# A graph layer on one core: where x is loaded and the bias added, the closing matmuls, and the order of the first sums and of layer 2's products

## The reference

```python
sums = segment_sum(edge_attr, src, n)
counts = segment_sum(ones, src, n)
agg = sums / maximum(counts, 1)[:, None]
combined = concatenate([x, agg, u[batch]], axis=1)    # 256 + 64 + 128
h = relu(combined @ W1 + b1)                          # 512
y = h @ W2 + b2                                       # 256
out = layernorm(x + y)
```

## Time and profile before

| | |
|---|---|
| median of 3 runs | 831.62 us (831.08 to 832.5) |
| profiled execution | 830.44 us |
| its span | 828.5 us |
| busy: PE, PEld | 763.8, 715.1 us |
| busy: DVE, ACT, POOL | 711.5, 539.7, 402.8 us |
| DMA | 156.37 MB, mean 189 GB/s |

### The profile page before, as it was taken

One profiled execution on the slowest core, in us unless ns is written; L12 is line 12 of the kernel. 1 busy time (PEld: TensorE's weight loads), 2 busy tenths in 40 slices (PEclk: granted clock), 3 DMA queues, 4 the chain that ended last, 5 costly groups with the idle time before them and its releaser, 6 DMA issues. The chain is left out here.

```text
span 828.5 us, 31441 instructions
## 1 busy us (share of the span) xinstructions
PE 763.8 (92%) x11398; PEld 715.1 (86%) x11399; DVE 711.5 (86%) x2317; ACT 539.7 (65%) x1128; POOL 402.8 (49%) x410
## 2 busy tenths in 40 slices
PE   9889999999989989998989978999999998899995
PEld 4689888888879888888888878999999997899995
DVE  8999999899988977987888707999999997799995
ACT  1356655666656646555656557888888885588886
POOL 3066666667666666656666660000000001598994
PEclk9999999999999999999999999999999999899999
DMA  6355555556656555555556448888888889711111
GB/s 206 130 193 195 197 188 195 201 179 203 200 182 202 184 187 184 190 187 185 189 187 181 161 151 278 267 262 260 265 262 258 265 259 242 171 53 61 63 62 63
DMA packets 74034, 156.37 MB, mean 189 GB/s; under 512 B 10851, under 2 KB 51044, under 8 KB 73239
## 3 DMA queue, kind: packets, MB, share of 16 engines
q1 hardware_dynamic: 57096, 102.33, 41.5%
q0 software_dynamic: 16896, 53.54, 17.2%
HBM read 95.47 MB, written 60.37 MB: 188 GB/s over the span
## 5 line engine op out<-in xcount | busy, mean ns | idle before, releaser
L604 POOL DMA_INDIRECT sorted_rows<-payload,idx x264 | 290.5, 1101 | 190.7 <-ACT payload L654 105.5
L867 PE MATMUL ps<-attr_buf,perm 128*128 128x198 bf16 x3168 | 308.8, 253 | 12.6 <-issue 8.4
L867 PEld LDWEIGHTS ps<-attr_buf,perm 128*128 128x128 bf16 x3168 | 287.8, 97 | 25.3 <-issue 18.7
L654 ACT CAST payload<-ps 128x792 bf16<-128x792 f32 x264 | 211.6, 832 | 146.0 <-PE ps L867 101.5
L1164 DVE TENSOR_SCALAR perm<-place_of,pos 128x512 bf16<-128x512 int16 x792 | 242.9, 365 | 23.3 <-PE ps L867 14.0
L1254 DVE TENSOR_SCALAR onehot<-node_of,sup 128x256 bf16<-128x256 int16 x838 | 183.3, 282 | 37.8 <-DMA sup<-sorted_rows 19.3
L949 PE MATMUL ps<-sup,onehot 128*128 128x64 bf16 (+1 forms) x6192 | 199.9, 193 | 5.2 <-issue 2.2
L949 PEld LDWEIGHTS ps<-sup,onehot 128*128 128x128 bf16 x6192 | 195.9, 97 | 9.2 <-issue 7.4
L624 POOL TENSOR_TENSOR xs<-xs,b_all 125x256 f32<-125x256 f32 x50 | 37.9, 782 | 203.8 <-DMA xs<-in_x 203.8
L722 ACT ACTIVATE apart<-node_of,sup 128x256 bf16<-128x256 int16 x194 | 96.6, 498 | 31.2 <-PE ps L949 30.2
L794 PE MATMUL ps<-xt,w1x 128*128 128x125 f32 x800 | 100.2, 279 | 2.9 <-ACT xt L659 2.5
(11 more groups left out here) (150 smaller groups left out, 606.8 us busy)
## 6 DMA issues: line engine op xcount, KB each, us to landing
sup<-sorted_rows SPq DMA_DIRECT2D x129, 396.0 KB, 4.0
attr_buf<-in_edge_attr SPq DMA_DIRECT2D x43, 576.0 KB
xs<-in_x SPq DMA_DIRECT2D x5, 1120.0 KB
out<-weights_z SPq DMA_DIRECT2D x25, 224.0 KB
x_stage<-in_x SPq DMA_DIRECT2D x47, 112.0 KB
sorted_rows<-payload,idx POOLq DMA_INDIRECT x264
pre<-jump_d SPq DMA_DIRECT2D x1, 1560.0 KB
pre<-first_d SPq DMA_DIRECT2D x1, 780.0 KB
```

The source lines that it names most:

```text
L604: pool.indirect_dma_start(out=sorted_rows, out_offset=bass.IndirectOffsetOnAxis(ap=idx[:, n:n + 1], axis=0), in_=payload[s][:, :], in_offs ...
L654: nc.scalar.copy(payload[s][:, :].rearrange("p (r w) -> p r w", w=PART), slots_p[s % PSUM_BUFS]).then_inc(s_pay, 1)
L867: last = nc.tensor.matmul(slot_p[s % PSUM_BUFS][r].rearrange("p (h f) -> p h f", f=PLANE), places, parts(a, t * CB + s), start=(t == 0 and ...
```

## The change

x goes into `xs` in twelve pieces of four columns and one of two. Each is loaded behind the super loads of one of SP's turns 3 to 15, whose loop is written out for it. POOL adds b2 to a piece as soon as it has landed, all 50 columns ahead of its first low part. The eight closing matmuls have one column each. PE runs 17 matmuls with zeros over 252 columns of bank 7 that hold no table, once two means are taken. Hidden sum 0 stands ahead of the means of banks 4 and 5, and the second split behind those of 2 and 3. Layer 2 computes the high products of both columns first and the low ones last, with one start and one stop for the bank.

```diff
--- before.py
+++ after.py
@@ -94,6 +94,8 @@
 PAIR_BUFS = 8
 HOT_BUFS = 4
 BODY = 2 * PAIR_BUFS
+UNUSED = 512 - (BUCKETS - (PAIR_BANKS - 1) * BANK_COLS) * ROW
+FILLERS = 17
 SUP_TURNS = SUPER_PAIRS // PAIR_BUFS
 PLACES_AT_ONCE = 4
 assert 2 * SUPER_PAIRS - SUP_TURNS * BODY <= PLACES_AT_ONCE
@@ -116,12 +118,12 @@
 LOOKS = -(-(BATCHES - SOON) // LOOK)
 assert LOOKS + 3 <= CHUNKS
 
-X_COLS = 10
+X_TURN = 3
+X_COLS = 4
 X_PIECES = COLS // X_COLS
 X_PIECE = X_COLS * DIM
-B2_AHEAD = 3
 Z_BUFS = 3
-assert X_PIECES * X_COLS == COLS and X_COLS % 2 == 0 and X_COLS // 2 >= B2_AHEAD
+assert X_TURN + X_PIECES + 1 == SUP_TURNS
 
 STEPS = COLS // 2
 PAIR = 10
@@ -319,6 +321,7 @@
         bias_p = bank(5, KH)
         pre_p = [bank(7, KH * NP), bank(1, KH * NP)]
         table_p = [bank(k, min(BANK_COLS, BUCKETS - k // 2 * BANK_COLS) * ROW) for k in range(BANKS)]
+        unused_p = bank(BANKS - 1, UNUSED, 512 - UNUSED)
         h_p = [ps[:, 2 * b * 512:(2 * b + 2) * 512] for b in range(2)]
         y_p = [bank(4 + b) for b in range(2)]
         aggt_p = [bank(6 + b, NW) for b in range(2)]
@@ -372,7 +375,7 @@
         s_apart = sem("s_apart")
         s_added = sem("s_added")
         s_table = sem("s_table")
-        s_xs = [sem(f"s_xs{k}") for k in range(X_PIECES)]
+        s_xs = [sem(f"s_xs{k}") for k in range(X_PIECES + 1)]
         s_xb = sem("s_xb")
         s_own_act = sem("s_own_act")
         s_own_dve = sem("s_own_dve")
@@ -526,15 +529,19 @@
                 sp.wait_ge(s_sent[s], 16 * CHUNKS)
 
             super_turn(0, found=True)
-            with sp.Fori(1, SUP_TURNS) as m:
+            for m in range(1, X_TURN):
                 super_turn(m)
-            super_turn(SUP_TURNS, SUPER_PAIRS - SUP_TURNS * PAIR_BUFS)
-
             sp.wait_ge(s_pre, COLS + 1)
             for k in range(X_PIECES):
+                super_turn(X_TURN + k)
                 for lo, hi in ((0, XPART), (XPART, NP)):
                     sp.dma_start(xs[lo:hi, k * X_PIECE:(k + 1) * X_PIECE], x_v[lo:hi, k * X_PIECE:(k + 1) * X_PIECE]
                                  ).then_inc(s_xs[k], 16)
+            super_turn(X_TURN + X_PIECES)
+            for lo, hi in ((0, XPART), (XPART, NP)):
+                sp.dma_start(xs[lo:hi, X_PIECES * X_PIECE:COLS * DIM], x_v[lo:hi, X_PIECES * X_PIECE:COLS * DIM]
+                             ).then_inc(s_xs[X_PIECES], 16)
+            super_turn(SUP_TURNS, SUPER_PAIRS - SUP_TURNS * PAIR_BUFS)
 
             def store_step(g, b):
                 sp.wait_ge(s_out, g * 2 + 2)
@@ -616,15 +623,11 @@
                 nc.gpsimd.tensor_tensor(low, whole, high.bitcast(F32), ALU.subtract).then_inc(s_w_lo, 1)
             pool.wait_ge(s_b2, 16)
 
-            def add_b2(g):
-                if g % (X_COLS // 2) == 0:
-                    pool.wait_ge(s_xs[g // (X_COLS // 2)], 2 * 16)
-                for c in range(2 * g, 2 * g + 2):
+            for k in range(X_PIECES + 1):
+                pool.wait_ge(s_xs[k], 2 * 16)
+                for c in range(k * X_COLS, min((k + 1) * X_COLS, COLS)):
                     column_x = xs[0:NP, c * DIM:(c + 1) * DIM]
                     nc.gpsimd.tensor_tensor(column_x, column_x, b2_all[0:NP, :], ALU.add).then_inc(s_xb, 1)
-
-            for g in range(B2_AHEAD):
-                add_b2(g)
 
             def low_hidden(g, b):
                 for c in range(2):
@@ -636,8 +639,6 @@
             pool.sem_inc(s_h_lo, 4)
             for g in range(STEPS):
                 low_hidden(g, g % 2)
-                if g + B2_AHEAD < STEPS:
-                    add_b2(g + B2_AHEAD)
 
         @block.scalar
         def _(act):
@@ -961,9 +962,11 @@
             find_tables(last_regs, SUP_TURNS * BODY)
             super_turn(SUP_TURNS, last_regs, 2 * SUPER_PAIRS - SUP_TURNS * BODY)
             for k in range(BANKS):
-                last = nc.tensor.matmul(table_p[k], zeros[:, :], zeros[:, 0:1].to_broadcast([P, table_p[k].shape[1]]),
-                                        start=False, stop=True)
+                last = nc.tensor.matmul(table_p[k][:, 0:1], zeros[:, :], zeros[:, 0:1], start=False, stop=True)
             last.then_inc(s_table, 1)
+            pe.wait_ge(s_agg, 2)
+            for k in range(FILLERS):
+                nc.tensor.matmul(unused_p, zeros[:, :], zeros[:, 0:1].to_broadcast([P, UNUSED]), start=True, stop=True)
 
             pe.wait_ge(s_w_lo, 2)
             pe.wait_ge(s_agg, 4)
@@ -998,8 +1001,8 @@
                     pe.wait_ge(s_agg, BANKS)
                 pe.wait_ge(s_h, g + 1)
                 pe.wait_ge(s_z, g * 2 + 2)
-                for c in range(2):
-                    for part in range(2):
+                for part in range(2):
+                    for c in range(2):
                         if part == 1:
                             pe.wait_ge(s_h_lo, g * 2 + (c + 1 + 4))
                         for k in range(KH):
@@ -1008,7 +1011,8 @@
                                 last = nc.tensor.matmul(y_p[b][0:NP, c * DIM:(c + 1) * DIM],
                                                         h_r[b][part][:, at:at + NP],
                                                         w2r[w_part][:, k * DIM:(k + 1) * DIM],
-                                                        start=(part == k == w_part == 0), stop=(part == 1 and k == KH - 1))
+                                                        start=(c == part == k == w_part == 0),
+                                                        stop=(c == part == 1 and k == KH - 1))
                 last.then_inc(s_y, 1)
 
             transpose_means(0, 0)
@@ -1340,11 +1344,13 @@
             for k in (6, 7, 0, 1):
                 mean(k)
             dve.wait_ge(s_agg, 4)
-            for q in range(2):
-                split_means(q)
-            for k in (2, 3, 4, 5):
+            split_means(0)
+            for k in (2, 3):
                 mean(k)
+            split_means(1)
             hidden_sum(0, 0)
+            for k in (4, 5):
+                mean(k)
             hidden_sum(1, 1)
             for g in range(STEPS):
                 step(g)
```

## The result

The changed kernel took 834.52 us in the median of 12 runs (828.42 to 840.67), the one before 832.32 (827.27 to 834.73): a ratio of 1.0056, interval 1.0029 to 1.0083 (the medians alone stand at 1.0026). The profiled execution had 832.38 us, its span is 829.1 (828.5 before): it is one of the quicker ones.

| us | before | after | forecast | measured |
|---|---|---|---|---|
| first product of the supers to the end of the last | 203.6 | 213.9 | +2.5 | +10.2 |
| from there to z(0) | 16.35 | 12.87 | -2.9 | -3.5 |
| z(0) to z(24), 24 steps | 105.86 | 101.91 | -3.6 | -3.95 |
| z(24) to the end | 6.5 | 6.5 | 0 | 0 |

The account below looks back on a forecast made before the run. PE's own pace was taken to bound the supers, and a two-step ring the steps behind. Terms -2.9 - 3.6 + 0.5 + 2.0 = -4.0 us gave a median of 827.6 us, range 822.5 to 835.

Parts of the forecast that it names:

- z(0): First residual sum of DVE, behind the supers: 2.9 us earlier in all, closing's 1.0 included (-1.7 to -3.5).
- The additions among the supers: POOL's 50 b2 additions beside DVE's one-hots: 28 us of DVE against 27 spare, +1, and +1 for bursts (0 to +10.5).
- The port rival: Supers, turns 3 to 15: additions shut DVE out 0.75 us each, making DVE the bound; +4.5 us, 836.1; chance 0.14.
- The port-free rival: Supers: POOL finds the port free while DVE waits for PE, nothing is lost; -6.5 us, 825.1; chance 0.18.
- The DMA: Residual input x loaded among the supers, 0.5 MB ahead of SP's later loads: +0.5 us (0 to +4).
- The rival's "0.86 + 0.18 is over 1": DMA late, in the supers: x pieces cut into super loads by 5 us; -1.5 us, 830.1; chance 0.10.
- Closing: Eight closing matmuls behind the supers with one column each: 1.40 us to 0.4, -1.0 (0 to -1.15).
- First sum: Hidden sum 0 ahead of two means, behind the supers: at 706.65 us, -1.35 (-1.0 to -1.75), closing included.
- The steps: 25 network steps: low products last and bias additions out, 4.41 to 4.26 us each, -3.6 (-1.5 to -5).
- a ring: Chain of two steps, z through statistics, hidden sum, ReLU, low part, layer 2 to z: 8.64 becomes 8.47 us.
- The rival of steps that do not get shorter: Network steps: the ring gives only its 0.17 us per two steps, 2 us; -2.4, 829.2; chance 0.16.
- Fillers: 17 PE matmuls behind the supers: 2.0 us, hardly holding the transposes; at half clock 3.6 us, holding them 1.6.

Follow-up runs that it names:

- e3: Changed kernel with each addition waiting for PE's progress, one every four supers from the fourth on; ratio 0.9986 to the kernel before, supers 208.7 us.
- e11: e5 with the additions one super later (13, 17, 21 and 25 supers from the start of their piece's turn); ratio 0.9929 to the kernel before.
- e12: Changed kernel, bursts of four additions kept, with eight one-hot buffers instead of four; ratio 0.9935 to the kernel before.
- e5: Changed kernel with one addition every four supers, the first only 12 supers into the turn; ratio 0.9951 to the kernel before.
- e2: Changed kernel with the 50 additions of b2 left out; ratio 0.9928 to the kernel before, turns of 12.38 us.
- e1: Changed kernel with the b2 additions back in the steps, x still loading among the supers; ratio 0.9992 to the kernel before.
- e4: Changed kernel with x loaded behind all supers and additions back in the steps, only the four tail parts kept; ratio 0.9977 to the kernel before.
- e10: e5 with the closing matmuls over all columns; ratio 0.9973 to the kernel before, z(0) at 14.34 behind.
- the six named above: Profiled executions with the changed kernel's order behind the supers where the clock fell once, to a mean of 0.88; z(0) at 14.39 to 14.71 behind.
- e9: e5 with all means and both splits ahead of hidden sum 0; ratio 0.9971 to the kernel before, z(0) at 13.57 behind.
- e8: e5 with layer 2 in the old order, high and low products of a column together; ratio 1.0009 to the kernel before.
- e6: e5 without the 17 filler matmuls; ratio 0.9950 to the kernel before.

## Why the prediction was wrong

It forecast 827.6 us, 4 under the kernel before; the ratio makes it 4.7 above. Between the profiled executions the span was to fall by 4.0 and rose by 0.6. That miss of 4.6 is +7.7 in the supers, -0.6 up to z(0), -0.3 in the steps, and -2.2 because the first product of the supers came earlier, which the change has no part in.

- **The additions among the supers: the step that failed.** "Spare are 13 turns x 1.9 and, once, the three supers built ahead, 2.3: 27 us. +1 and [...] +1 more" measured +11.0 over the twelve turns with a full burst (159.5 us instead of 148.5), +10.2 on the whole stage. The cost of one addition was right, even somewhat high (0.49 us of DVE against the 0.55). The account was wrong in kind. It pooled DVE's spare time over all turns against the sum of the losses. But PE is the bound of this stage: what it loses in a burst it does not get back when DVE has time again (its turns never fall under the 12.3 to 12.4 us they have without additions), and what counts is each burst against the lead at that moment. Four additions take 2.0 us from DVE and PE lost 0.92; three (e3) 0.4; one by one at the right place, nothing (e11). In e12, with the bursts untouched and a longer lead, nearly nothing. The clause on the burst that "eats the whole lead" saw the cause and priced it once instead of twelve times.
- **The port rival**, with a chance of 0.14, had the sign and a loss of 10.5 us in the supers by the full 0.75 us for each addition. That its number came near is luck, since each addition did not cost 0.75: PE's loss came by another way. By the Trainium skill, "SBUF — State Buffer", section "Who interferes with whom", whoever comes second blocks until the other is finished. The trace agrees for single operations (one-hots of 0.77 us beside additions of 0.72), and shows what the rule leaves open: under a steady stream the two take turns, one one-hot for each addition. Who came second can't be read from the recorded starts: in e5 and e11 a delayed one-hot often starts up to 0.04 us ahead of its addition in the record (0.85 us beside 0.73) and still ends 0.08 behind it.
- **The port-free rival** leaves out the forecast's own +0.5 for the DMA: -2.9 - 3.6 + 0.5 is -6.0, not -6.5. e2, where the additions are left out, came at -6.0 by its ratio.
- **The DMA**: the forecast took +0.5 of 0 to +4; e1 and e2 show 0. A super load landed in 4.5 us instead of 4.0, inside the cover of 5. The rival's "0.86 + 0.18 is over 1" priced x too high: in e1 the share of a turn of 12.38 us rose from 0.86 to 0.98, by 0.12, at 309 GB/s. The forecast's 230 GB/s came from rows of 10 KB, while the pieces now have rows of 4 KB. In e4, where such pieces load with no super beside them, the stretch from 714 to 722 has 268 GB/s at a share of 1.04. That is one run, on another chip, so that the length of the rows is the reason is likely and not shown.
- **Closing**: -1.0 forecast (0 to -1.15), 1.2 measured (e10 against e11). Right, just past the bound.
- **First sum**: -1.35 with the closing; in the profile it starts 6.2 us behind the last super instead of 8.2, -2.0, beyond the bound of -1.75. The clock stayed up in this execution. Where it fell, in the six named above, the sum starts 7.5 to 7.8 us behind, only -0.4 to -0.7, short of the bound of -1.0. The order itself is worth 0.45 (e9).
- **z(0)**: -2.9 forecast, -3.5 measured, bound -3.5. How near it came is luck with the clock: in the six executions in which it fell, z(0) came 1.9 to 2.2 us earlier than in the one trace of the kernel before, in the four others 3.5.
- **The steps**: 4.26 forecast, 4.246 measured; 8.47 a ring, 8.46 measured. Right, and by its two terms: the order alone leaves 4.40 (e4) or 4.37 (e1), the additions' absence alone 4.32 (e8), both 4.25. The rival of steps that do not get shorter falls.
- **Fillers**: "they are 3.6 us and hold them 1.6" at the low clock is what e5 shows (3.64).

## What to carry to other kernels

Work put beside a stage that runs at one engine's pace is not paid from the spare time of the others in sum, but burst by burst from the buffers between them: a helper that shuts the producer out for t must stay under the lead at that moment, or the bound engine loses the rest for good. So spread it by the consumer's own progress (here one wait on PE's count before each addition, worth 1.3% by the ratios of e11 and the changed kernel), or lengthen the lead. And where two reasons hold a ring at its length, each removed alone shows less than its share: here 0.01 to 0.04 us a step by the order, 0.09 by the additions, and 0.16 by both together.

## What the runs showed of the hardware that was not expected

- Where the additions stand counts beside how many stand together. Each alone, at supers 0, 4.4, 8.4 and 12.5 of a turn they cost PE 0.2 us in most turns, always at super 14.5, where PE reads the table places of the next supers; one super later they cost nothing (e5 against e11, 12.60 and 12.39 us a turn). The stop isn't there when the addition at 12.5 is the turn's only one, and it is missing in some turns with all four (turn 14 of e5 at 12.43 us, turns 8 and 12 of e6 at 12.38 and 12.39). Why it falls on that read was not tried.
- GpSimd and DVE alternate under load: in the bursts of the changed kernel the additions stand 0.69 us apart, and for each one exactly one one-hot is stretched, from 0.28 to 0.76 us, and ends 0.08 to 0.09 behind it.
- The DMA engines can be at a share of 0.98, with 309 GB/s, and hold up nothing: in e1 x and the supers share them and a turn still takes 12.38 us. The x loads at 10 KB a row alone kept them at a share of 1.03 with 230 GB/s before.
